# A softmax's row maxima are subtracted on GpSimd instead of VectorE, and its exponentials move from lag 9 to lag 10

## The reference

```python
xn = layernorm(x)                                   # eps 1e-5, no gain
q, k, v = split(xn @ Wqkv.T + bqkv, 3)              # 512 columns each
# 16 heads of 32; attention runs over the FIRST axis: the 8 rows n of one b
scores = mask + 32 ** -0.5 * einsum('bnd,bmd->bnm', q, k)
out = einsum('bnm,bmd->bnd', softmax(scores), v)
y = x + (out @ Wproj.T + bproj) + (fp8(xn) @ fp8(Wffn).T + bffn)
```

## Time and profile before

| | |
|---|---|
| median of 3 runs | 1623.73 us (1623.5 to 1623.75) |
| profiled execution, device time | 1623.51 us |
| its span in the trace | 1621.7 us |
| busy: TensorE / VectorE / GpSimd / ScalarE | 1503.6 / 1512.6 / 1265.4 / 1032.9 us |

### The profile page before, as it was taken

The page is one execution under the profiler, slowest core; times in us unless marked ns, Lnnn a source line. Parts: engine busy times, 40 slices in busy tenths (PEclk is TensorE's granted clock), DMA queues, the critical chain, the costliest instruction groups (busy, mean ns, idle before and its releaser), DMA issues.

```text
span 1621.7 us, 24736 instructions
## 1 busy us (share of the span) xinstructions
PE 1503.6 (93%) x6791; PEld 677.0 (42%) x6913; DVE 1512.6 (93%) x1316; ACT 1032.9 (64%) x1946; POOL 1265.4 (78%) x854
## 2 busy tenths in 40 slices
PE   4997999999999999999999999999999999999955
PEld 3443443444444444444444444444444444444412
DVE  7499999999999999999999999999999999999992
ACT  5666667666666666666666676666766666676422
POOL 1367979788797978879797887979788796978775
PEclk8999999999999999999999999999999999999978
DMA  5343544545454554545445454544545454454333
GB/s 196 74 100 77 129 109 112 130 103 132 101 128 109 116 132 101 124 104 136 103 116 129 103 130 102 131 108 113 127 103 136 104 125 114 102 137 90 95 76 80
DMA packets 366502, 184.06 MB, mean 113 GB/s; under 512 B 314160, under 2 KB 314160, under 8 KB 366384
## 3 DMA queue, kind: packets, MB, share of 16 engines
q1 hardware_dynamic: 366384, 182.53, 46.3%
HBM read 73.41 MB, written 33.55 MB: 66 GB/s over the span
## 4 chain that ended last, share of the span: by engine, by line
POOL 43%; issue 29%; DVE 10%; PE 7%; ACT 1%; POOLq 1%; DMA 0%; SPq 0%; DVEq 0%; ACTq 0%
POOL prod_pv L381 28%; DVE prod_qk L687 5%; POOL xs L420 5%; POOL x L410 4%; POOL o L399 3%; DVE scores L691 2%; POOL rstd L405 2%; POOL probs L392 2%; PE k_ps L572 2%; PE v_ps L572 2%; PE proj_ps L572 1%; PE q_ps L572 1%; DVE stats L715 1%; POOLq L74 1%; PE lin_ps L610 0%
## 5 line engine op out<-in xcount | busy, mean ns | idle before, releaser
L381 POOL TENSOR_TENSOR prod_pv<-kv,probs 128x2048 f32<-128x2048 f32 x192 | 699.4, 3642 | 16.2 <-POOL probs L392 11.1
L724 DVE TENSOR_REDUCE o_nat<-prod_pv 128x512 f32<-128x2048 f32 (+1 forms) x128 | 429.1, 3353 | 27.0 <-POOL prod_pv L381 16.7
L691 DVE TENSOR_REDUCE scores<-prod_qk 128x64 f32<-128x2048 f32 x192 | 439.4, 2288 | 7.3
L687 DVE TENSOR_TENSOR prod_qk<-q_ps,kv 128x2048 f32<-128x2048 f32 x192 | 432.0, 2250 | 2.5 <-ACT kv L527 2.5
L572 PE MATMUL k_ps<-wqkv_hi,xT 128*128 128x512 f16 x1024 | 328.0, 381 | 49.4 <-DMA xT<-x 47.6
L572 PE MATMUL proj_ps<-wproj_hi,oT 128*128 128x512 f16 x1032 | 334.7, 386 | 4.9 <-ACT proj_ps L520 4.9
L572 PE MATMUL q_ps<-wqkv_hi,xT 128*128 128x512 f16 x1024 | 325.4, 379 | 0.0
L572 PE MATMUL v_ps<-wqkv_hi,xT 128*128 128x512 f16 x1024 | 325.4, 379 | 0.0
L399 POOL TENSOR_TENSOR o<-o_nat,o 128x512 f16<-128x512 f32 x128 | 148.6, 1161 | 199.0 <-ACT o L484 199.0
L536 ACT ACTIVATE kv<-v_ps 128x512 f32<-128x512 f32 x128 | 141.8, 1108 | 171.3 <-PE v_ps L572 145.5
L572 PE MATMUL proj_ps<-wproj_lo,oT 128*128 128x512 f16 x516 | 200.3, 388 | 0.0
(11 more groups left out here) (115 smaller groups left out, 1694.4 us busy)
## 6 DMA issues: line engine op xcount, KB each, us to landing
xn<-in_L_attn_x SPq DMA_DIRECT2D x128, 256.0 KB, 2.8
xs<-in_L_attn_x SPq DMA_DIRECT2D x128, 256.0 KB, 2.9
out<-xs SPq DMA_DIRECT2D x128, 256.0 KB, 2.2
xT<-x SPq DMA_TRANSPOSE x256, 3.0
kv<-in_L_attn_Wqkv SPq DMA_DIRECT2D x3, 1024.0 KB, 10.8
oT<-o SPq DMA_TRANSPOSE x128, 3.2
kv<-in_L_ffn_weight SPq DMA_DIRECT2D x1, 1024.0 KB, 5.5
kv<-in_L_attn_Wproj SPq DMA_DIRECT2D x1, 1024.0 KB, 14.7
```

Source lines behind the costliest of these rows:

```text
L381: nc.gpsimd.tensor_tensor(o, v, p, ALU.mult).then_inc(pv_multiplied, 1)
L687: nc.vector.tensor_tensor(prod_qk[:, :].rearrange("p (m c) -> p m c", c=C), qb, k, ALU.mult).then_inc(qk_multiplied, 1)
L691: nc.vector.tensor_reduce(scores[:, :, m0:m0 + 4].rearrange("p h m -> p m h"), prod_qk[:, :].rearrange("p (m h d) -> p m h d", h=H, d=D), ...
L724: nc.vector.tensor_reduce(o_nat[:, n % 2, :], prod_pv[:, place:place + units, :].rearrange("p q (c m) -> p c q m", m=4), AX_XY, ALU.add).t ...
```

## The change

GpSimd does the subtraction, in its own slot, after the first unit of products. The maxima go to SBUF, and `scores`, `shifted` and the maxima have two places, for even and odd tiles. The exponentials, their sum and its reciprocal are taken at lag 10 (`L_SOFT`), and the subtraction at lag 9 (`L_SHIFT`). The presetting of a q bank waits for the last product with the q before, as the maxima no longer lie there. VectorE's score sums wait for the subtraction of two tiles before instead of one.

```diff
-L_STATS, L_CENTRE, L_NORM, L_KV, L_Q, L_QK, L_SOFT, L_PV, L_SUM, L_RES, L_SPLIT, L_LIN, L_PROJ = \
-    1, 2, 3, 4, 5, 8, 9, 11, 12, 12, 13, 14, 15
+L_STATS, L_CENTRE, L_NORM, L_KV, L_Q, L_QK, L_SHIFT, L_SOFT, L_PV, L_SUM, L_RES, L_SPLIT, L_LIN, L_PROJ = \
+    1, 2, 3, 4, 5, 8, 9, 10, 11, 12, 12, 13, 14, 15
...
-        scores = sb("scores", [P, H, N], F32)
-        shifted = sb("shifted", [P, H, N], F32)
+        scores = sb("scores", [P, 2, H, N], F32)
+        row_max = sb("row_max", [P, 2, H], F32)
+        shifted = sb("shifted", [P, 2, H, N], F32)
...                                      # GpSimd, after the first unit of products
+                if live(i, j, L_SHIFT):
+                    n = j - L_SHIFT
+                    keys = keys_of(n)
+                    after(pool, max_ready, tile_count(i, n))
+                    after(pool, exps_ready, tile_count(i, n - 2))
+                    nc.gpsimd.tensor_tensor(shifted[:, n % 2, :, 0:keys], scores[:, n % 2, :, 0:keys],
+                                            row_max[:, n % 2, :].unsqueeze(2).broadcast_to([P, H, keys]),
+                                            ALU.subtract).then_inc(shifted_ready, 1)
...                                      # ScalarE
-                after(act, shifted_ready, tile_count(i, n - 4))
+                after(act, qk_multiplied, unit_count(i, last_unit(n - 4)))
                 nc.scalar.activation(q_ps[n % 4][:, :], q_bias[:, :], ACT.Copy).then_inc(q_preset, 1)
...                                      # VectorE
-                after(dve, shifted_ready, tile_count(i, n - 1))
+                after(dve, shifted_ready, tile_count(i, n - 2))
...
-                    row_max = q_ps[n % 4][:, 0:H]
                     after(dve, qk_reduced, unit_count(i, last_unit(n)))
-                    after(dve, qk_multiplied, unit_count(i, last_unit(n)))
-                    nc.vector.tensor_reduce(row_max, scores[:, :, 0:keys], AX_X, ALU.max).then_inc(max_ready, 1)
-                    after(dve, max_ready, tile_count(i, n))
-                    after(dve, exps_ready, tile_count(i, n - 1))
-                    nc.vector.tensor_tensor(shifted[:, :, 0:keys], scores[:, :, 0:keys],
-                                            row_max.unsqueeze(2).broadcast_to([P, H, keys]),
-                                            ALU.subtract).then_inc(shifted_ready, 1)
+                    nc.vector.tensor_reduce(row_max[:, n % 2, :], scores[:, n % 2, :, 0:keys], AX_X,
+                                            ALU.max).then_inc(max_ready, 1)
```

More of the change, by code:

```diff
@@ L465, in slot @@
                     after(act, probs_ready, tile_count(i, n - 4))
-                    nc.scalar.activation(exps[:, n % 4, :, 0:keys], shifted[:, :, 0:keys], ACT.Exp,
+                    nc.scalar.activation(exps[:, n % 4, :, 0:keys], shifted[:, n % 2, :, 0:keys], ACT.Exp,
                                          scale=exp_scale[:, 0:1]).then_inc(exps_ready, 1)
@@ L689, in scores_of_unit @@
                 after(dve, qk_multiplied, unit_count(i, u))
-                after(dve, shifted_ready, tile_count(i, n - 1))
-                nc.vector.tensor_reduce(scores[:, :, m0:m0 + 4].rearrange("p h m -> p m h"),
+                after(dve, shifted_ready, tile_count(i, n - 2))
+                nc.vector.tensor_reduce(scores[:, n % 2, :, m0:m0 + 4].rearrange("p h m -> p m h"),
                                         prod_qk[:, :].rearrange("p (m h d) -> p m h d", h=H, d=D), AX_X,
```

## The result

The changed kernel took 1643.39 us (median of 4 runs, 1640.88 to 1644.59), the kernel before 1623.74 beside it: a ratio of 1.0116, interval 1.0103 to 1.0128. It is 1.2% slower, and 32.7 us above the forecast of 1610.7. The profiled execution took 1644.59, its span 1642.8.

A forecast was written before the change was run, and what follows sets the result against it. The prediction took VectorE's own work as the bound, with GpSimd touching it once in two groups. From 1623.5 us it took 35.8 saved, added 25.6 of new waits and removed 2.6 of old ones: 1610.7 us, range 1600 to 1621.

The forecast's parts named there:

- VectorE's saving: On VectorE: 128 subtractions removed save 0.32 us with 8 keys and 0.25 with 4, 35.8 us in all.
- GpSimd's subtraction: On GpSimd: 128 subtractions, rows like its probabilities' 0.407 and 0.301 us, taken as 0.37 and 0.26 after overlap.
- The maxima in SBUF: On VectorE: writing maxima to SBUF changes each by 0.04 us less to 0.04 more, 5 us in all; nothing taken.
- The chain: Reciprocal of slot 0 through GpSimd to o_nat in slot 3: 23.06 us, so VectorE waits 1.92 or 1.49; 25.6 us.
- some 25 us in 15 places and not 16.7 in 13: Sign in VectorE's waits: o_nat waits for GpSimd's products, each in a slot 3 and 1.5 to 1.9 us long.
- The sum: Whole kernel: 1623.5 less 35.8 saved, plus 25.6 of new waits, less 2.6 of replaced waits, gives 1610.7 us.
- The start and the tail I leave as they are, with 2 us either way: Outside the loop passes: start and tail taken as unchanged, with 2 us either way.
- The whole saving: Rival: the chain has unseen cover and VectorE stays without a gap, 1585.1 us; chance 0.10.
- The ring over TensorE: Rival: TensorE and transposes waiting behind the store close a ring, 93.3 us against 94.4 a group; 1618 to 1624; chance 0.18.
- The dear subtraction: Rival: GpSimd's small subtraction, twice in the chain, loses the gain from 0.69 us; 1637.7 us at 1.16; chance 0.10.
- The rule that spoke against the change: On GpSimd: about twice as slow for two-input elementwise work, a 4-key subtraction of 0.44 us, 1614.9 instead of 1610.7.

The follow-up runs named there:

- e10: e6 with its 28 padding instructions moved under VectorE's idle wait in slot 5 of the start: 1584.24 us, 0.9749 of the kernel before.
- e9: Changed kernel with 28 padding instructions under VectorE's idle wait in slot 5 of the start, its loop at 205: 1611.56 us, 0.9920 of the kernel before.
- e3: e1 with GpSimd's second unit of products moved ahead of the low part of the output: 1604.0 us, 0.9875 of the kernel before.
- e7: e1 with SyncE's store moved behind the three transposes, nothing else: 1609.15 us, 0.9905 of the kernel before.
- e5: Changed kernel with the subtraction back on VectorE, lag 10 and two places kept, loop at 205: 1625.41 us, 1.0007 of the kernel before.
- e1: Changed kernel with 28 instructions of already met waits in VectorE's slot 2, moving its loop back to 205: 1613.85 us, 0.9935 of the kernel before.
- e11: e6 without the 28 padding instructions: 1603.91 us, 0.9872 of the kernel before.
- e2: Kernel before with 100 instructions of already met waits in VectorE's slot 2, moving its loop to 305: 1656.29 us, 1.0195 of the kernel before.
- e6: e3 with SyncE's store moved behind the three transposes, last in its slot: 1585.71 us, 0.9759 of the kernel before.
- e4: Kernel before with only the exponentials, their sum and reciprocal at lag 10, one place for shifted: 1714.86 us, 1.0556 of the kernel before.

## Why the prediction was wrong

**What held.** VectorE's saving: 12.78 us for a long slot (809.10 to 821.87 in the changed kernel) where it was 13.11, so 0.33 for a forecast of 0.32. A slot 0 is 10.25 (821.87 to 832.12) where it was 10.55 (814.21 to 824.76), and in e10, where no products are late, slots 1 and 2 are 10.25 and 10.18 where they were 10.46 each; the three save 0.26 on the mean, for a forecast of 0.25. GpSimd's subtraction cost 407 and 299 ns, as its probabilities do; its groups by line and shape:

```profile
L402 POOL TENSOR_TENSOR shifted<-scores,row_max 128x128 f32<-128x128 f32 x64 | 26.0, 407 | 8.0 <-DVE row_max L757 8.0
...
L402 POOL TENSOR_TENSOR shifted<-scores,row_max 128x64 f32<-128x64 f32 x64 | 19.1, 299 | 0.1
```

The maxima in SBUF took 286 and 163 ns, 8 or 9 less than in PSUM, inside the estimate of 40. The chain of products is late in slot 3 by 1.91 and 1.60 (1.92 and 1.49 forecast), and in e9, without the stall, by 1.90 to 1.92 and 1.60 to 1.92. And where the loop stands as it did before, the whole sum comes out: e9 took 1611.56 against 1610.7, with a pass of 188.60 against 188.8. As e3 removes the slot-3 gaps by order alone, e7 leaves them, and e5 has the smaller ones worked out for it, the mechanism of "The chain" is shown.

That e9 comes so near is in part luck. Its late products are 40.1 us, and the forecast implies 39.7 (16.7 - 2.6 + 25.6), but the parts differ. In slot 3 it has 25.6 us in 14 places, 1.83 on the mean, where 15 of 1.70 were forecast; a fifteenth gap, of 2.0 us in the tail, is put down to "issue". In slot 2 it has 3.3 us that nobody forecast. Everywhere else it has 11.2, where the kernel before had 14.1. The prediction's sign of "some 25 us in 15 places and not 16.7 in 13" also forgot the 14.1 that its own sum leaves in place.

**The step that failed** is "The sum". It is made of VectorE's saving and the late products alone, and puts the loop's return at nothing, without a reason: a pass was to take 188.8 us and took 194.06. Of the rest it says "The start and the tail I leave as they are, with 2 us either way". The tail did stay (141.1 for 142.2). The start was read for its time alone. But taking out the subtractions and moving the softmax a lag later shortens VectorE's program ahead of the loop by 28 instructions, and with the loop at that place each return waits until VectorE's instructions are fetched again. That has no term in the sum and no rival. It cost 1643.4 - 1611.6 = 31.8 us (changed kernel against e9): some 22.4 as idle time at "issue" (24.4 - 2.0), 8.7 as products that are late more often (48.8 - 40.1), the rest not assigned. e1, e9 and the pair e10 and e11 take the stall away by moving the loop only, and e2 brings it into the kernel before.

How the stall makes products late is less firmly shown. In the trace, GpSimd's probabilities in slot 1 wait 3.37 to 4.47 us for VectorE's reciprocal after each of the six returns (41.5 us of such waits in all, 21.9 in e9), TensorE's transposed x comes late by 3.81 to 4.87, the granted clock falls to 0.50 for 3 to 7 us behind that, and in the following group GpSimd is late in slots 1 and 2 as well. Without the stall, in e9, all of it is gone or small: at these places the probabilities don't wait, the transposed x is late by 0.36 to 0.38, the clock stays at 1.00, and some 0.25 remain in slot 2. Neither the stall nor the lower clock is enough for late products: e2 and e11 have both, the clock at 0.50 behind five and four of their six returns, and their products are late no more than without (16.5 and 0.4 us). Of the three kernels with the stall only the changed one, with its own order on GpSimd, has more late products. How much of the 8.7 us is the clock's and how much the slots' shift wasn't separated.

The Trainium skill has the rule in question ("Runtime: NRT & Kernel Launch", section Instruction fetch mechanics): a taken branch whose target isn't among the two pages of instructions that the engine holds waits for a DMA fetch. The trace agrees that a return can stall, 4.07 us in the row above. The page gives pages of 256 instructions, two to an engine. By that, and if the pages are counted from the start of VectorE's program, the loop at 177, which ends at 495, would lie in two pages and be held, and the one of before, 205 to 569, would need three and be fetched. The runs show the opposite (80 packets and 50, and none of the 50 keeps VectorE's time in the passes). The packets of q14 have 8 KB where the page has 16 KiB; only those of the other queue, q8, have 16 (1.11 MB in 68). Here the runs decide.

**The rivals.** The whole saving (1585.1) had its own reason against it and that reason held: it took two other orders to get there, 1585.7 in e6 and 1584.2 in e10. The ring over TensorE isn't what holds the loop at its old place: e7 opens it and the gaps of slot 3 stay. The dear subtraction (1637.7) lies nearest to the measured time, but its mechanism is refuted by the 299 ns. That it came near is an accident.

**The rule that spoke against the change** (the Trainium skill, "GPSIMD Engine Reference", section 4.1, a factor of two) gave 1614.9 in the prediction. The subtraction took 299 / 221 = 1.35 and 407 / 288 = 1.41 times VectorE's, so the rows were the better guide, and e9's 1611.56 lies nearer to their sum.

## What to carry to other kernels

An edit to an engine's program can have a price that no instruction row shows: what it does to the place of the loop. Look at the number of instruction packets and at the idle time called "issue" ahead of the first instruction of a pass, before and after; if both rise, move the loop by some instructions under a wait at the start before judging the change itself. And when a wait of a chain is taken away, look at once for the transfer that stands in a queue behind the same chain: here the load of x, which had the store and three transposes ahead of it. 18 of the 28 us came only when the transposes went ahead of the store.

## What the runs showed of the hardware

- A loop of 319 to 368 instructions on VectorE returns in 0.3 to 0.4 us at one place, and in 2.8 to 4.6 us at another 28 instructions earlier or 100 later. The first instruction stands at 205 in nine of the kernels and at 201 in e4, all with 50 packets; at 177 in two and at 305 in one, all with 80. The rule behind it is open, since only these four places were tried.
- ScalarE's loop of 451 or 455 instructions goes with five instruction packets of 8 KB in every pass, in each of the 13 kernels, wherever VectorE's loop stands.
- 56 waits that are already met, built as 28 instructions, cost 2.6 us where nothing covers them, and 200, built as 100, cost 10.1: about 0.1 us for each instruction built.
- TensorE's granted clock fell to 0.50 for 6 us after a wait of 4.33 us, and didn't with 0.37 at the same place. Between 200 and 1500 us it fell behind each of the changed kernel's six returns and never in the kernel before, e1, e3 or e5 to e10. At 0.50 matmuls of 512 columns start 0.42 us apart instead of 0.22.
